# A four-layer modulated convolution in quads of samples: the second quad's H by a blurred M, T(1) behind the first B product, the ze read behind the blur, the last quad by halves

## The reference

```python
TYPES = ('same', 'upsample', 'same', 'downsample')
s = style @ mw.T + mb
weight = SCALE * w * s[:, None, :, None]
demod = lax.rsqrt(jnp.sum(weight * weight, axis=(2, 3)) + EPS)
weight = weight * demod[:, :, None, None]
# same: conv(x, weight) + b;  upsample: blur(conv_transpose(x, weight, stride 2) + b)
# downsample: conv(blur(x), weight, stride 2) + b;  blur kernel (1, 3, 3, 1) / 8
return x + layer3(layer2(layer1(layer0(x))))
```

## Time and profile before

| what | us |
|---|---|
| median of 3 runs | 169.03 |
| the runs | 167.65, 169.82, 169.03 |
| the profiled execution | 167.63 |
| its span | 165.6 |
| busy: TensorE / VectorE / ScalarE / GpSimd | 147.6 / 113.4 / 91.6 / 74.7 |

### The profile page before, as it was taken

How to read it: one execution, slowest core, us unless ns; L and a number is a source line. 1 busy time by engine, 2 the same in 40 slices (tenths; PEclk the granted TensorE clock), 3 DMA queues, 4 the chain that set the end, 5 groups by cost and what they waited for, 6 DMA issues and landing times.

```text
span 165.6 us, 5479 instructions
## 1 busy us (share of the span) xinstructions
PE 147.6 (89%) x2353; PEld 104.0 (63%) x2353; DVE 113.4 (68%) x183; ACT 91.6 (55%) x181; POOL 74.7 (45%) x98
## 2 busy tenths in 40 slices
PE   7789999999998199989998999899989999969930
PEld 5366896866565047646876667676758765648830
DVE  7758626997779930799189728955992799391460
ACT  3316387447174118384859666857768485833430
POOL 7300039599980196950690096029304920950000
PEclk9965699999999869999999999999999999999996
DMA  4959000051001500007940980295055008206326
GB/s 130 351 137 246 29 4 0 4 199 60 0 4 46 208 6 0 4 0 273 352 143 8 224 279 4 63 236 216 2 114 145 4 0 187 70 4 149 108 55 198
DMA packets 9735, 17.64 MB, mean 107 GB/s; under 512 B 4752, under 2 KB 5360, under 8 KB 9712
## 3 DMA queue, kind: packets, MB, share of 16 engines
q1 hardware_dynamic: 9424, 16.98, 35.3%
q10 hardware_dynamic: 288, 0.33, 0.7%
HBM read 8.91 MB, written 8.39 MB: 105 GB/s over the span
## 4 chain that ended last, share of the span: by engine, by line
PE 60%; DVE 20%; issue 7%; ACT 5%; DMA 3%; ACTq 1%; DVEq 1%
PE p_c L611 22%; PE p_h L593 12%; PE p_k L556 6%; DVE H_sb L1085 5%; PE p_k L542 5%; DVE H_sb L1088 4%; PE p_k L572 3%; DMA w1n<-in_L_cond_weights_dram 3%; DVE w_sb L1078 3%; DVE w_sb L1082 2%; ACT M_sb L839 2%; DVE H_sb L1091 2%; ACT w_sb L839 2%; PE p_h L469 1%; DVE d_sb L1058 1%
## 5 line engine op out<-in xcount | busy, mean ns | idle before, releaser
L1110 DVE TENSOR_TENSOR p_c<-p_c,s_sb 128x1024 f32<-128x1024 f32 x13 | 16.0, 1233 | 25.8 <-PE p_c L611 22.1
L611 PE MATMUL p_c<-dd_sb,Tw 64*64 64x256 f32 (+1 forms) x512 | 28.4, 369 | 0.0
L883 ACT ACTIVATE ot<-p_c,pvec 128x508 f32<-128x508 f32 x26 | 20.5, 863 | 9.1 <-PE p_c L611 9.1
L611 PEld LDWEIGHTS p_c<-dd_sb,Tw 64*64 64x64 f32 x512 | 21.2, 133 | 6.8 <-issue 1.9
L593 PE MATMUL p_h<-H_sb,W_st 64*64 64x448 f32 (+1 forms) x192 | 20.4, 555 | 4.1 <-DVE ze L974 3.8
L243 POOL TENSOR_TENSOR Tw<-Tw,di_sb 128x128 f32<-128x128 f32 x7 | 3.2, 456 | 41.4 <-ACT Tw L848 41.3
L263 POOL TENSOR_TENSOR dx_sb<-xin 128x1032 f32<-128x1032 f32 x8 | 19.8, 2476 | 2.3 <-issue 2.2
L611 PE MATMUL p_c<-d_sb,Tw 64*64 64x256 f32 x320 | 19.8, 386 | 0.0
L611 PE MATMUL p_c<-dx_sb,Tw 64*64 64x256 f32 x320 | 18.9, 375 | 0.0
L1058 DVE TENSOR_TENSOR d_sb<-xin 128x2072 f32<-128x2072 f32 x8 | 18.5, 2309 | 0.0
L1066 DVE TENSOR_TENSOR dd_sb<-d_sb 128x2064 f32<-128x2064 f32 x8 | 18.4, 2301 | 0.0
(11 more groups left out here) (172 smaller groups left out, 258.7 us busy)
## 6 DMA issues: line engine op xcount, KB each, us to landing
xin<-in_x_dram SPq DMA_DIRECT2D x16, 512.0 KB, 5.3
out_dram<-ot SPq DMA_DIRECT2D x14, 512.0 KB, 6.3
out_dram<-ot SPq DMA_DIRECT2D x3, 256.0 KB, 3.6
out_dram<-ot ACTq DMA_DIRECT2D x1, 256.0 KB, 4.5
wn<-in_L_cond_weights_dram SPq DMA_DIRECT2D x1, 192.0 KB, 3.6
mwn<-in_L_cond_mod_w_dram SPq DMA_DIRECT2D x1, 128.0 KB, 2.2
xe<-in_x_dram SPq DMA_DIRECT2D x2, 64.0 KB, 9.1
w1n<-in_L_cond_weights_dram ACTq DMA_DIRECT2D x1, 48.0 KB, 4.8
```

The lines of the kernel that those rows point to most:

```text
L611: ins = pe.matmul(bank[j * C:(j + 1) * C, i], Tw[q % NW][rows, blk, j, :], moving(rows, j, n), start=(first and n == 0), stop=(n == len(bl ...
L883: act.activation(ot[q % NO_T][:, i, 4 + par:4 + par + 2 * n - 1:2], bank[:, i, 2:2 + n], ACT.Identity, bias=pcol(W_C, 2 * q + i), scale=pc ...
L1110: dve.tensor_tensor(bank[:].rearrange("p i (n h) -> p i n h", h=2), p_a[:, :, w * NQ:(w + 1) * NQ].unsqueeze(3).to_broadcast([P, 2, NQ, 2] ...
```

## The change

Six things change:

1. Prologue. H(1) is no longer composed on TensorE; M(1) is composed right behind H(0) into bank p_x, which is free there, and VectorE blurs it. H_sb has two buffers. d(0) is made earlier on VectorE. The two `keep_busy(1)` go, and the matmuls of the blurred taps are placed later; the load of w1n is issued ahead of two small ones.
2. T(1) stands behind bc2(0), no longer ahead of it. a2(0) goes to bank p_h.
3. VectorE reads ze right behind blur_M(2), ahead of d(1) and dd(1).
4. In every blur the two short operations that read the bank come ahead of the last long one, with a signal of their own (M_read); R(q+2) waits for M_read, T(q+1) for H_made, which now comes from the long one.
5. a2(7) does not wait for y02 of quad 6; bc2(7) does.
6. The last quad: a13(7) writes two banks, bc3(7) and bc1(7) are both made in halves and interleaved, and VectorE and ScalarE take their operations in another order.

```diff
-            return p_b if q + 1 < QUADS else p_h
+            return p_b if 0 < q < QUADS - 1 else p_h
+
+        def bank_M(q):
+
+            return p_k if q > 1 else p_x
...
         def bank_bc3(q):
-            return p_a if not alone(q) else p_k if q + 2 == QUADS else p_h
+            return p_k if alone(q) else p_a
...
-            def keep_busy(times):
-
-                for _ in range(times):
-                    pe.matmul(p_h[:, 1, 0:256], pe_warm[:, 0:P], pe_warm[:], start=True, stop=True)
-
             pe.wait_ge(warm_made, 1)
-            keep_busy(4)
+            for _ in range(4):
...
             blurred_taps(p_h[:, 0], p_y[:, 0], 0)
-            blurred_taps(p_h[:, 0], p_y[:, 0], 1)
...
-            blurred_taps(p_h[:, 0], p_y[:, 0], 2).then_inc(put["FT"], 1)
+            blurred_taps(p_h[:, 0], p_y[:, 0], 1)
...
-            pe.wait_ge(made["bias"], 1)
-            keep_busy(1)
+            blurred_taps(p_h[:, 0], p_y[:, 0], 2).then_inc(put["FT"], 1)
...
-            keep_busy(1)
...
-                    pe.wait_ge(H_evac, 4)
+                    pe.wait_ge(T_evac, 2)
                 elif q > 2:
-                    pe.wait_ge(H_made, q - 2)
+                    pe.wait_ge(M_read, 2 * (q - 1))
...
-                pe.wait_ge(T_evac, 4 * q - 2)
+                if q > 1:
+                    pe.wait_ge(T_evac, 4 * q - 2)
...
-                if q < 2:
-                    pe.wait_ge(H_evac, 2 * (q + 1))
+                if q == 0:
+                    pe.wait_ge(H_evac, 2)
                 else:
-                    pe.wait_ge(H_made, q - 1)
+                    pe.wait_ge(H_made, q)
                 wait(pe, T_evac, 4 * q)
+                if q == 1:
+                    pe.wait_ge(t_made, 2)
...
-                wait(pe, y02_made, 2 * q)
+                wait(pe, y02_made, 2 * q if q + 1 < QUADS else 0)
...
             def product_bc2(q):
                 pe.wait_ge(dx_made, q + 1)
                 if q == 0:
-                    pe.wait_ge(t_made, 2)
+                    pe.wait_ge(M_read, 2)
                 elif q + 1 < QUADS:
                     pe.wait_ge(seeded, 2 * q)
+                else:
+                    pe.wait_ge(y02_made, 2 * q)
...
+            def last_products():
+
+
+                q = QUADS - 1
+                pe.wait_ge(d_made, q + 1)
+                pe.wait_ge(seeded, 2 * q)
+                pe.wait_ge(T_sums, 3 * QUADS)
+                part(q, half(p_k, 0), (B_U + 1, B_U + 3), odd(q, 1), first=False).then_inc(a13_done, 1)
+                part(q, half(p_a, 0), (B_U, B_U + 2, 0), odd(q, 0), first=False).then_inc(a13_done, 1)
+                pe.wait_ge(dd_made, q + 1)
+                for h in range(2):
+                    of = slice(h * NQ // 2, (h + 1) * NQ // 2)
+                    if h == 1:
+                        pe.wait_ge(e1_made, q + 2)
+                    bank = bank_y13(h)[:, :, 0:NQ]
+                    part(q, parity(bank, 0), (7, 3), second(q, 1, 0, of))
+                    part(q, parity(bank, 1), (5, 1), second(q, 1, 1, of), first=False).then_inc(bc3_done, 1)
+                    if h == 0:
+                        pe.wait_ge(e1_made, q + 1)
+                    else:
+                        pe.wait_ge(e_scaled, 2 + 2 * 2)
+                    bank = bank_y02(h)[:, :, h * NQ:(h + 1) * NQ]
+                    part(q, parity(bank, 0), (8, 4, 0), second(q, 0, 0, of), first=False)
+                    part(q, parity(bank, 1), (6, 2), second(q, 0, 1, of), first=False).then_inc(bc1_done, 1)
 
             p_e = p_h[:, 0]
...
-            compose_H(0)
-            pe.wait_ge(copied["W1_st"], 1)
+            pe.wait_ge(copied["G_mv"], 1)
             pe.wait_ge(made["vec"], 1)
             for k in range(K):
-                ins = pe.matmul(p_x[0:C, 1, 256:256 + B], wn[:, 1, :, k], vec[0:C, V_B0, 0:B], start=(k == 0),
+                ins = pe.matmul(p_y[0:C, 1, 256:256 + B], wn[:, 1, :, k], vec[0:C, V_B0, 0:B], start=(k == 0),
                                 stop=(k == K - 1))
             ins.then_inc(put["yc"], 1)
-            pe.wait_ge(copied["G_mv"], 1)
+            compose_H()
+            compose_M(1)
+            pe.wait_ge(made["yc"], 1)
             blurred_halves(3, p_y[:, 1], cid1, 3).then_inc(put["oT"], 1)
             compose_T(0)
             pe.wait_ge(made["z_st"], 6)
-            pe.wait_ge(made["yc"], 1)
+            pe.wait_ge(copied["o_st"], 1)
             for k in range(3):
-                ins = pe.matmul(p_x[:, 1, 0:B], z_st[:, k, :], yc[:], start=(k == 0), stop=(k == 2))
+                ins = pe.matmul(p_y[:, 1, 288:288 + B], z_st[:, k, :], yc[:], start=(k == 0), stop=(k == 2))
             ins.then_inc(put["zc"], 1)
-            compose_H(1)
             edge_x0()
             pe.wait_ge(made["zc"], 1)
-            pe.wait_ge(copied["o_st"], 1)
             for k in range(3):
                 for h in range(2):
...
-                if q + 1 < QUADS:
+                if 0 < q < QUADS - 1:
                     compose_T(q + 1)
                 product_bc2(q)
                 if q == 0:
+                    compose_T(1)
                     pe.wait_ge(made["e_read"], 2)
                     pe.wait_ge(made["c"], 2)
+                if q + 1 == QUADS:
+                    last_products()
+                    break
                 product_a13(q)
...
+            act.dma_start(w1n[C:P], weights[1]).then_inc(w1_loaded, 16)
             act.dma_start(bn[0:LAYERS], mod_b).then_inc(b_loaded, 16)
             act.dma_start(bn[LAYERS:2 * LAYERS], biases).then_inc(b_loaded, 16)
-            act.dma_start(w1n[C:P], weights[1]).then_inc(w1_loaded, 16)
...
-                wait(act, M_done, q - 3)
-                if 2 <= q < 4:
-                    act.wait_ge(H_done, q - 1)
+                wait(act, H_done, 1 if q > 1 else 0)
+                wait(act, M_done, q - 2)
...
+                elif q + 1 == QUADS:
+                    for bank in (p_k, p_a):
+                        act.activation(bank[:, :, 0:NQ], bank_a2(q)[:, :, 0:NQ], ACT.Copy).then_inc(seeded, 1)
...
-            evac_H(0)
+            make_x3(0)
+            evac_H()
+            evac_M(1)
             act.wait_ge(put["oT"], 1)
             copy(o_st[:], p_y[:, 1, 0:3 * C].rearrange("p (a c) -> p a c", c=C), copied["o_st"], 0.125)
-            make_x3(0)
             act.wait_ge(made["s0"], 2)
             evac_T(0)
             make_A(2)
-            evac_H(1)
...
+                if q + 1 == QUADS:
+                    scale_s(q)
                 if q > 0:
                     evac_s(q)
-                if alone(q):
+                if q + 2 == QUADS:
...
+            def blur_ends(q):
+                odd, even = odd_and_even(q)
+                n = 5 * (q - 1)
+                wait(dve, T_done, q - 1)
                 dve.wait_ge(blurred, n + 4)
-                dve.scalar_tensor_tensor(out=H_sb[:], in0=w_sb[:, :, 1:NH + 1], scalar=14.0, in1=w_sb[:, :, 0:NH],
+                dve.scalar_tensor_tensor(out=H_sb[q % 2][:], in0=w_sb[:, :, 1:NH + 1], scalar=14.0, in1=w_sb[:, :, 2:NH + 2],
                                          op0=ALU.mult, op1=ALU.add).then_inc(blurred, 1)
-                dve.wait_ge(blurred, n + 5)
-                dve.tensor_tensor(H_sb[:], H_sb[:], w_sb[:, :, 2:NH + 2], ALU.add).then_inc(blurred_twice, 1)
-                dve.wait_ge(blurred_twice, q - 1)
                 for i in range(2):
-                    ins = dve.scalar_tensor_tensor(out=H_sb[:, i, 2:5], in0=odd[i], scalar=pcol(W_A64, 2 * q + i),
-                                                   in1=H_sb[:, i, 2:5], op0=ALU.mult, op1=ALU.add)
-                ins.then_inc(H_made, 1)
+                    dve.wait_ge(blurred, n + 5)
+                    dve.scalar_tensor_tensor(out=w_sb[:, i, 2:5], in0=odd[i], scalar=pcol(W_A64, 2 * q + i),
+                                             in1=w_sb[:, i, 2:5], op0=ALU.mult, op1=ALU.add).then_inc(M_read, 1)
+
+                dve.wait_ge(M_read, 2 * q)
+                h = H_sb[q % 2]
+                dve.tensor_tensor(h[:], h[:], w_sb[:, :, 0:NH], ALU.add).then_inc(H_made, 1)
+
...
+                scaled_e(q, p_k, 0, slice(0, m))
+                unscaled_e(0)
+                unscaled_e(1)
+                scaled_e(q, p_k, m, slice(m, NQ))
+                outputs(0)
+                outputs(1)
...
+            dve.wait_ge(made["a0"], 2)
+            ts(pvec[:, W_A6], pvec[:, W_A0], 6.0, name="a6")
+            ts(pvec[:, W_A64], pvec[:, W_A0], -64.0, name="a6")
...
+            make_d(0)
+            blur_begins(1)
             dve.wait_ge(put["zc"], 1)
-            tt(zc[:], p_x[:, 1, 0:B], vec[:, V_E2, 0:B], ALU.mult)
+            tt(zc[:], p_y[:, 1, 288:288 + B], vec[:, V_E2, 0:B], ALU.mult)
             then()
             tt(zc[:], zc[:], vec[:, V_SB2, 0:B], ALU.add, "zc")
             dve.wait_ge(ident2_made, 1)
             dve.wait_ge(made["id"], 2)
             add_ident(dve, 0)
             sum_blocks(dve, 0)
-            make_d(0)
```

(6 more changed lines are left out.)

160 lines of the change are left out of this document (77 added, 83 removed).

## The result

| | before | after |
|---|---|---|
| median, us | 169.43 (4 runs, 167.65 to 170.55) | 156.6 (4 runs, 156.41 to 158.49) |
| profiled execution, its span | 167.63, 165.6 | 156.41, 154.5 |
| ratio of the times | | 0.930, 95% interval 0.918 to 0.942 |

The change makes the kernel 7% faster. I had forecast 159.0 us with a range of 156.8 to 162.2: the median lies 2.4 us under the forecast and 0.2 us under the low end of the range. Before has one run more here than in the front part, and its median is 0.40 us higher; the ratio of 0.930, set against the 169.03 us that I forecast from, gives 157.2 us, just inside the range.

The account below looks back on a forecast made before the run. TensorE's list was taken as the bound, busy 147.6 of 165.6 us. The terms 5.5 + 2.2 + 0.2 + 1.4 - 0.6 = 8.7 us gave a span of 156.9 and a median of 159.0, range 156.8 to 162.2.

Parts of the forecast that it names:

- The ze read: Ahead of T(2): reading ze right behind the blur removes 3.82 us of wait and 1.70 of slow clock, 5.5 us.
- The order inside the blur: In every blur: R needs only M_read, so its five waits go without T waiting instead; 2.2 us, bounds 1.5 and 2.2.
- GpSimd behind it: After the ze read: edge adds meet long VectorE operations and dx(2) runs beside blur(3); 0.6 us lost, bounds 0 and 2.3.
- The prologue: Start to ye: TensorE loses 5 us of work, but the clock, VectorE and GpSimd leave only 0.2 us gained.
- I expect the clock to rise at the same time: Prologue: slow clock still ends with R(0) and R(1) just ahead, so H(0) keeps 0.8 of over 2 us.
- M(1) ahead of T(0) turns this into about 0.6 us of delay: Prologue: M(1) standing before T(0) turns H(0)'s 0.8 us of earlier start into about 0.6 us of delay.
- It starts when it did: Prologue: GpSimd's chain of y_st and x0e, which releases ye at 41.45, starts unchanged, so ye cannot start much earlier.
- The tail: Last quad: a2(7) earlier, products in halves, TensorE ending about 1.0 us earlier; 1.4 us gained, bounds 1.0 and 1.8.
- The clock falls in the new gap: Rival, ahead of a2(0): the 1.2 us idle stretch lowers the clock, costing 1.7 us, time 160.7; chance 0.14.
- The lock decides: Rival, prologue and quad 2: new long VectorE operations meet GpSimd's work, costing about 2.3 us, time 161.2; chance 0.14.
- The change doesn't do what it says: Rival: T(2) still waits because H(2) or ze is late; time 165.2, within 2%; chance 0.05.
- slower: Rival: without keep-busy matmuls the clock stays at 1.2 GHz into the loop, about 28 us beyond 19.5; chance 0.02.

Follow-up runs that it names:

- b_ze: Kernel before with VectorE's ze read alone moved behind blur(2) of quad 0, ahead of d(1): 165.12 us, ratio 0.983.
- a_ze_back: Kernel after with the ze read alone put back behind d(1) and dd(1): 162.1 us, ratio 0.966.
- b_mread: Kernel before with the order inside the blur alone changed and R waiting for M_read: 168.07 us, not distinguishable from before.
- a_a2_waits: Kernel after in which a2(7) waits for y02 of quad 6 again: 157.89 us, ratio 0.947.
- b_combo: Kernel before with the early part of the prologue, the ze read and the order inside the blur: 158.51 us, ratio 0.940.
- b_early: Kernel before with w1n loaded ahead of the two small loads, later blurred taps and no keep-busy matmuls: 165.51 us, ratio 0.981.
- a_d2_late: Kernel after with VectorE's d(2) moved from between dd(1) and the two e of quad 1 to behind blur(3): 156.59 us, ratio 0.940.
- a_busy: Kernel after with the two pairs of keep-busy matmuls put back into the prologue: 158.85 us, ratio 0.943.

## Why the prediction was right or wrong

**The ze read: right.** I had 3.82 us of wait and 1.70 of slow clock. M(3) came 5.91 us earlier against ye, with 0.28 of R(3)'s wait in it, so 5.6. T(2) stood right behind R, and the clock stayed at full. b_ze and a_ze_back give 5.2 and 6.1 for the same stretch. That d(1) and dd(1) come later cost nothing on TensorE, as forecast.

**The order inside the blur: right.** I took 2.2 us, the sum of five waits. b_mread gives 2.45 over four quads, a little more than the 2.2, since it also ends small pauses that the list of waits does not name.

**GpSimd behind it: right in kind, too small.** I charged 0.6 us with bounds of 0 and 2.3. The debt is 1.34 us in after (a_ze_back) and 1.7 in b_ze. The mechanism is the one in the text: long ze adds, dx(2) beside blur(3), a blur operation of over 2 us, a wait ahead of T(3) of 0.47, under the 1 us that I named as the sign of more. The step that failed is that I charged the first meeting alone. In after a late dx makes VectorE late, so that a later dx meets a later blur: R(5) waits 0.49 too. (T(7)'s 0.28 was 0.24 before.)

**The prologue: wrong, 0.2 us forecast and 2.30 measured; this is most of the miss.** Three steps failed, one behind the other.
First, "I expect the clock to rise at the same time". In before it is at 0.50 from 9.26 to 19.50. In after it fell at 8.1 and rose between 18.30 and 18.40:

```profile
8.00:18.30 10.30, 9.80 (x112) 8.52 (x112) 7.89 (x38) 4.86 (x16) 0.08 (x1) 0.51 0.66 174
18.30:39.15 20.85, 20.00 (x342) 16.23 (x337) 18.45 (x34) 11.80 (x27) 16.96 (x20) 1.00 0.17 61
```

I had tied the end of the slow stretch to R(0) and R(1), and nothing in the trace spoke for that. From R(0)'s start to the rise 2.3 us passed in before and 3.9 in after, and over all eight profiles whose record shows the rise 2.2 to 5.0. Nor does it follow the products ahead of it: the first ones behind the load of w1n start at 6.37 or 6.38 us in five profiles with after's early part, and the clock fell there between 7.7 and 9.4 and rose between 16.2 (a_a2_waits) and 19.2 (b_combo):

```profile
9.40:16.20 6.80, 6.80 (x87) 6.25 (x84) 5.18 (x26) 2.92 (x9) 0.00 (x0) 0.50 0.82 181
```

```profile
8.96:19.20 10.24, 10.24 (x121) 9.22 (x125) 7.31 (x35) 5.04 (x16) 0.70 (x4) 0.50 0.61 150
```

What sets the time of the rise is not shown here; it is not a fixed point. The products ahead of R(0) themselves came earlier: those behind the load by 0.70 us (6.37 and not 7.07), those of line 495, ahead of which fewer taps stand, by 1.23, and those behind the pairs that went by more. So H(0) starts at 18.71, 1.99 us earlier, and not 0.8.
Second, "M(1) ahead of T(0) turns this into about 0.6 us of delay". From H(0) to T(0) after takes 4.97 us and before 4.07, so M(1) costs 0.90 and I had 1.4. M(1) takes 1.62 us there, but the six small products of line 746, which stood behind H(0), now stand ahead of it (0.3), and from the start of line 468's products to T(0) it is 0.80 us where it was 1.22. T(0) came 1.09 us earlier.
Third, "It starts when it did", of GpSimd's chain. That followed from the first two. The chain itself was right: it sets ye, and is 8.71 us long, where the earlier trace rows has 9.27. It starts 1.74 us earlier with the block sums. I had counted 5 us of TensorE work as gone and then argued nearly all of it away; b_early shows that 2.1 of it arrive at ye, with no help from M(1).

The pair of profiles may also understate the gain: 12.8 us lie between the medians and 11.1 between the spans. Before's profiled run is the earliest at H(0) of the three with that prologue, so the runs of before may lose in the prologue what its profile doesn't show. This is not shown, since the other runs have no traces.

**The tail: right in kind, 0.5 us too small.** bc2(7) came 1.2 us earlier (I had 1.6): y02 of quad 6 was itself 0.53 us late for it. TensorE ended 0.71 us earlier (I had 1.0), and the last store was issued 1.09 us earlier (22.67 behind T(7), before 23.76), where I had 1.4 for VectorE's last operation. But the end of the span moved by 1.94. The term that was mis-sized is the stores: I had them start earlier and no longer queue, but gave nothing for their landing, and from the last issue to the end it took 4.65 us instead of 5.50.

**The rivals.** *The clock falls in the new gap* did not happen in the profiled run of after, but in two of eight profiles with this gap, at 1.26 us and not the 1.7 that I took. It is a property of single runs and may be part of the spread of after's runs (156.41 to 158.49); this wasn't measured. *The lock decides* did happen to some extent, in quads 2 to 6, where it costs 1.3 us. In the prologue it took nothing at ye that it had not taken before. There the Trainium skill (SBUF — State Buffer, "Who interferes with whom") has the rule that a VectorE instruction with two inputs from SBUF and a GpSimd instruction that reads SBUF exclude each other. The trace agrees as to single operations: y_st's adds had 724, 1456 and 1511 ns, the two long ones beside blur(1). I had written that by that rule the term would be the loss. That inference was wrong: in before y_st was held as well, by d(0) (one add of 2730 ns), so the holding only changed its partner. The price of this rival was added up wrongly as well: 1.4 and 1.7 are 3.1 us, and half of both is 1.6, not 2.3. *The change doesn't do what it says* and *slower* fell with the first row of T(2), and with the clock back at 18.3 without any keep-busy product.

**The range.** Its low end, 156.8, came from 0.6 us for the best prologue. With the measured 2.3 the same working gives 155.1 as the low end. The bound was not a bound: it rested on the one sentence about the clock. That the other stages together came within 0.3 us of my sum is in part luck: the tail gave 0.5 more, the loop 0.4 less.

## What to carry over

The end of a slow-clock stretch in a prologue is not fixed to the products that stand at it: with one and the same early part it came between 16.2 and 19.2 us. A bound on a prologue must let it move, and two profiles should be compared from an event behind it (here H(0)), not from the start. Products that only keep TensorE busy should be tried without, first: here they cost 1.1 us in the trace and 1.1% by the ratio (0.2 to 2.0%), and put back into after they cost 2.3 us in the medians. Where a stall goes away on the busiest engine, look at GpSimd and VectorE in the next three quads, and not only in the next: what one held operation makes late is held again there.

## What the runs showed of the hardware that I had not expected

**The granted clock ahead of its first change can't be read off.** In b_early the window of the eight products at line 492 says 1.00, and so does after's window of the same eight products (line 495):

```profile
7.97:9.03 1.06, 1.06 (x11) 1.00 (x10) 0.91 (x3) 0.00 (x0) 0.00 (x0) 1.00 1.03 421
```

```profile
7.31:7.96 0.65, 0.65 (x13) 0.61 (x10) 0.54 (x3) 0.00 (x0) 0.00 (x0) 1.00 0.99 372
```

The same products take 1.06 and 0.65 us, and in b_early those behind them go on at the pace that after has at 0.50 (R(0)'s 21 matmuls take 2.12 us in both). So the clock was low at that time already, and the record doesn't say so. The same products take 1.06 us, under a record of 1.00, in b_ze, b_mread, a_ze_back, a_d2_late and a_busy. Durations decide. The prologue differs from profile to profile by this and by when the clock rises; T(0) in the profiles of kernels with after's early part lies between 22.39 and 24.70 us.

**The clock fell behind an idle stretch of 0.85 us in two profiles of eight** with such a gap ahead of a2(0), and stayed up behind 1.67 us ahead of a2(7) in each of seven. Ahead of T(2), with 3.8 to 4.7 us idle, it fell in each of the five profiles that have the gap. Length alone doesn't decide it; what does isn't shown.

**GpSimd and VectorE hold each other up in both directions.** GpSimd's ze add takes 0.47 us free and 2.42 to 2.47 beside a d of VectorE; VectorE's long blur operation takes 1.09 free and up to 2.9 beside a dx. GpSimd's copy of x0e takes 0.56 us in before and 2.73 in after, where dd(0) of VectorE starts with it. GpSimd's busy time rose from 74.7 to 85.8 us with no operation added.
